# Graph attention layers: GpSimd multiplies the third head's rows of every second group, in place of VectorE

## What is computed

```python
xl = (x @ Wl + bl).reshape(n, h, d)
xr = (x @ Wr + br).reshape(n, h, d)
e = jax.nn.leaky_relu(xl[src] + xr[dst], NEG_SLOPE)
score = jnp.einsum('ehd,hd->eh', e, att)
m = jax.ops.segment_max(score, dst, num_segments=n)
ex = jnp.exp(score - m[dst])
denom = jax.ops.segment_sum(ex, dst, num_segments=n)
alpha = ex / denom[dst]
out = jax.ops.segment_sum(alpha[:, :, None] * xl[src], dst, num_segments=n)
```

## Time and profile before

| | us |
|---|---|
| time, median of 3 runs (lowest to highest) | 6554.96 (6551.42 to 6558.74) |
| the profiled execution, its own time | 6546.25 |
| span in its profile | 6544.4 |
| first graph attention layer, about | 1636 to 3290 |
| second graph attention layer, about | 3390 to 5100 |

### The profile page before, as it was taken

How to read it: one execution, slowest core, us unless ns; L and a number is a source line. 1 busy time by engine, 2 the same in 40 slices (tenths; PEclk the granted TensorE clock), 3 DMA queues, 4 the chain that set the end, 5 groups by cost and what they waited for, 6 DMA issues and landing times. The chain is left out here.

```text
span 6544.4 us, 130007 instructions
## 1 busy us (share of the span) xinstructions
PE 4986.5 (76%) x23046; PEld 2906.8 (44%) x23047; DVE 5557.6 (85%) x13086; ACT 4324.9 (66%) x19265; POOL 3959.7 (61%) x3547
## 2 busy tenths in 40 slices
PE   3796899842888889888878899889998645555663
PEld 2573455421444444444463444444444435555552
DVE  9999988732999999999857999999999547777777
ACT  5576799720899999999837999999999430000001
POOL 0588877785666666666405666666665017777774
PEclk9999999966999999999989999999999767777776
DMA  0362000132555555555515555555556024444444
GB/s 13 62 81 22 2 2 2 11 53 52 146 139 139 140 139 139 140 139 140 100 41 144 140 140 140 139 141 141 139 139 128 23 67 127 127 126 126 126 126 73
DMA packets 397652, 656.25 MB, mean 100 GB/s; under 512 B 141767, under 2 KB 259461, under 8 KB 397044
## 3 DMA queue, kind: packets, MB, share of 16 engines
q0 software_dynamic: 185888, 481.62, 29.0%
q1 hardware_dynamic: 211540, 172.59, 11.3%
HBM read 617.73 MB, written 33.88 MB: 100 GB/s over the span
## 5 line engine op out<-in xcount | busy, mean ns | idle before, releaser
L1272 POOL DMA_INDIRECT feat_area<-xl_table,feat_area x1856 | 2007.0, 1081 | 1476.7 <-PE bank L1346 668.4
L1423 ACT ACTIVATE feat_area<-feat_area 128x130 f32<-128x130 f32 x5568 | 1643.5, 297 | 237.2 <-DVE feat_area L1476 234.0
L1333 PE MATMUL bank<-node_area,feat_area 128*128 x3712 | 1472.3, 520 | 339.4 <-DVE feat_area L1468 174.4
L1407 ACT ACTIVATE feat_area<-feat_area 128x128 f32<-128x128 f32 x4640 | 1442.1, 387 | 30.7 <-issue 30.7
L1346 PE MATMUL bank<-feat_area 128*128 128x390 f32 x3712 | 1408.9, 502 | 33.7 <-ACT feat_area L1407 12.6
L634 POOL DMA_INDIRECT rec_by_dst<-feat_area,gather_col x800 | 1051.2, 1314 | 243.7 <-issue 233.1
L1856 POOL DMA_INDIRECT feat_area<-kv_table,feat_area x832 | 829.4, 997 | 562.3 <-DMA feat_area<-gather_src 309.0
L1333 PEld LDWEIGHTS bank<-node_area,feat_area 128*128 128x128 f32 x3712 | 634.7, 190 | 988.8 <-issue 731.1
L1423 ACT ACTIVATION_READ_ACCUMULATOR feat_area<-feat_area 128x1 f32 x5568 | 1040.2, 187 | 0.0
L1346 PEld LDWEIGHTS bank<-feat_area 128*128 128x128 f32 x3712 | 670.2, 190 | 601.6 <-issue 196.0
L1468 DVE TENSOR_TENSOR feat_area<-bank,feat_area 128x780 f32<-128x780 f32 x928 | 889.6, 959 | 24.4 <-DMA feat_area<-xl_table,feat_area 17.8
(11 more groups left out here) (320 smaller groups left out, 6823.2 us busy)
## 6 DMA issues: line engine op xcount, KB each, us to landing
feat_area<-lo_slot SPq DMA_DIRECT2D x464, 128.0 KB, 3.3
feat_area<-xl_table,feat_area POOLq DMA_INDIRECT x1856, 3.4
feat_area<-lo_slot_src SPq DMA_DIRECT2D x208, 128.0 KB, 3.3
node_area<-lo_edge SPq DMA_DIRECT2D x100, 256.0 KB
xl_table<-feat_area SPq DMA_DIRECT2D x98, 195.0 KB, 3.3
feat_area<-kv_table,feat_area POOLq DMA_INDIRECT x832, 3.0
rec_by_dst<-feat_area,gather_col POOLq DMA_INDIRECT x800
feat_area<-gates SPq DMA_DIRECT2D x348, 32.0 KB
```

The lines of the kernel that those rows point to most:

```text
L1272: pool.indirect_dma_start(ring[:, at:at + HE], None, k.xl, bass.IndirectOffsetOnAxis(ap=index[s // CG][:, n:n + 1], axis=0)).then_inc(gath ...
L1333: last = nc.tensor.matmul(pair[s % 2][:, u, 0:HE], pick[s // 2 % 2][:, c:c + P], k.node[:, ds(columns[0], HE)], start=True, stop=True)
L1407: last = nc.scalar.activation(row[:, 0:D], row[:, 0:D], ACT.Copy, scale=row[:, D:D + 1])
L1423: last = nc.scalar.activation(at, at, ACT.Copy, accum_out=score[s // CG][:, to:to + 1])
```

## The change

VectorE's step `weight` goes, and the same multiplication, on the same rows, is written as a second step of GpSimd's stream with the same lead of -11. GpSimd waits for `weights` there, and raises `byvec`. VectorE's list loses the entry and is otherwise as before.

```diff
-            pipeline(pool, groups, [(0, gather)], U)
+            def weight(j, s):
+                if s % 2:
+                    return
+                pool.wait_ge(weights, chunk(j, s) + 1)
+                pool.nop(nofuse=True)
+                rows = ring4[:, s * GS:(s + 1) * GS, H - 1, :]
+                nc.gpsimd.tensor_tensor(rows[:, :, 0:D], rows[:, :, 0:D], rows[:, :, D:D + 1].to_broadcast([P, GS, D]),
+                                        ALU.mult).then_inc(byvec, 1)
+
+            pipeline(pool, groups, [(0, gather), (-11, weight)], U)
...
-            def weight(j, s):
-                if s % 2:
-                    return
-                dve.wait_ge(weights, chunk(j, s) + 1)
-                rows = ring4[:, s * GS:(s + 1) * GS, H - 1, :]
-                nc.vector.tensor_tensor(rows[:, :, 0:D], rows[:, :, 0:D], rows[:, :, D:D + 1].to_broadcast([P, GS, D]),
-                                        ALU.mult).then_inc(byvec, 1)
...
-                                   (-2, carry), (0, weigh), (-2, spread_fwd), (-3, spread_weights), (-11, weight),
+                                   (-2, carry), (0, weigh), (-2, spread_fwd), (-3, spread_weights),
```

## The result

The changed kernel takes 7185.1 us (median; 7182.1 to 7187.5), the kernel before, run beside it, 6553.6 us: a ratio of 1.097, 95% interval 1.0956 to 1.0983. It is slower by some 631 us. The forecast was 7145 us in a range of 6930 to 7450.

The account below looks back on a forecast made before the run. VectorE was taken to bound the kernel, with ScalarE close behind. A net loss of 3.99 us plus 1.2 of late effects per chunk, over 114 chunks, made 593 us: about 7145 us, in a range of 6930 to 7450.

Parts of the forecast that it names:

- The deciding term: GpSimd's in-order stream: it stands 8.9 us per chunk for the weights, holding group 220's gathers; VectorE loses 5.35 us.
- First leg: From VectorE's weights copy to the addition of the chunk's 12th group after its first: 6.95 us in place of 1.60.
- the gap before it: On GpSimd, between the weights being there and its multiplication: 0.30 us.
- The landing: From the end of a group's second gather on GpSimd to VectorE's addition: 3.1 us, between 2.12 and 3.77.
- What comes late next: TensorE at half clock after idling, and GpSimd starting the chunk late: together 1.2 us per chunk, of 0 to 2.5.
- The part ascribed to GpSimd starting late: GpSimd needs 32.1 us per chunk against VectorE's 31.4, nearly level, so small waits would appear.
- What VectorE gives up: VectorE loses four multiplications of 0.34 us per chunk, 1.36 us, 158 us in all, all on the path.
- The sum: Net 3.99 plus 1.2 gives 5.2 us per chunk, paid by 114 chunks: 593 us, about 7145 us in all.
- the second term: The late effects on TensorE's clock and GpSimd's start, 1.2 us per chunk, added to the net 3.99.
- GpSimd as the bound: Rival: GpSimd's load sets the pace from about 2.8 us a group; 7390 us at 3.1; chance 0.23.
- The two engines in each other's way: Rival: VectorE and GpSimd exclude each other on SBUF reads, up to 3.3 us per chunk, about 7520; chance 0.05.
- Signs that were named: One GpSimd idle stretch per chunk, 114 gather waits of 4 to 6 us, VectorE's busy time down about 80 us per layer.

Follow-up runs that it names:

- wait_only: The kernel before, VectorE keeping its multiplication; GpSimd only waits for the weights at the place of the change's multiplication: 8213.8 us, ratio 1.100.
- lead14: The changed kernel with GpSimd's multiplication three groups later in its stream: 7491.6 us, ratio 1.0027 to the kernel before.
- after_here: The changed kernel, unchanged, run again on another chip: 7181.3 us, ratio 1.0979 to the kernel before there.
- filled2: The changed kernel with five more matmuls of no use on TensorE over the wait, beside the changed kernel on the same chip: 7090.6 us, ratio 1.0832.
- no_mult: The kernel before without the multiplication of the third head's rows in even groups, on any engine: 7383.2 us, ratio 0.9889.
- all14: The changed kernel, multiplication three groups later and on GpSimd in every group, odd ones in place of ScalarE: 7673.3 us, ratio 1.0105 to the kernel before.
- lead13: The changed kernel with GpSimd's multiplication two groups later in its stream: 7610.7 us, ratio 1.0035 to the kernel before.
- work_only: The kernel before, VectorE keeping its multiplication, plus 464 GpSimd multiplications on data of its own without waiting for weights: 7642.9 us, ratio 1.0234.
- lead12: The changed kernel with GpSimd's multiplication one group later in its stream: 7933.0 us, ratio 1.0462 to the kernel before.
- before_here: The kernel before, unchanged, profiled on a slower chip of the experiments: 7482.5 us in one run, 27.58 and 27.70 us per chunk.
- filled: The changed kernel with five more matmuls of no use on TensorE over the wait, on a slower chip: 8268.5 us, ratio 1.0892.

## Why the prediction was right

**The deciding term held.** GpSimd stood 8.7 us before the multiplication of a chunk (8.9 forecast), and VectorE paid for it at one group per chunk. wait_only has the loss with no work, lead14 has the work and next to no loss (0.27%).

**First leg, the sum of 6.95 us.** Measured 6.47 in the mean. In the chunk shown: 0.23 + 0.15 + 0.62 + 0.18 + 1.08 + 0.31 + 0.95 + 2.66 = 6.18. Two terms were sized too high: the multiplication (0.82; it takes 0.62) and the gap before it (0.30; 0.15). The landing, 2.90 us in the mean over a layer's 57 such gathers, was near the 3.1 taken.

**What comes late next, 1.2 us of 0 to 2.5.** This was the mis-sized term. With all of the 1.36 us granted, leg two is 7.76 where 6.62 - 0.34 = 6.28 was due, 1.5 us more, most of it the clock as the fill of the pipeline had shown (1.85 there; 1.1 by after_here and filled2). Leg three is 18.89 where 19.33 - 1.02 = 18.31 was due: 0.6 more. Together 2.1, not 1.2; the 0.6 is about what no_mult gives back too little. The part ascribed to GpSimd starting late was small in the change itself (38 us of waits at other groups than the fifth, 17 before) and came out only when the clock no longer hid it.

**What VectorE gives up, 1.36 us.** It was priced too high, and that "all of it" is on the path did not hold: on its own it is worth 0.76 us (no_mult), with ScalarE close behind VectorE. In the changed kernel it can't be separated from leg three.

**The sum.** +5.2 us per chunk forecast, +5.6 and +5.8 measured; too little in the second term, too much in the first and in the landing, so that the 7145 came within 40 us of 7185 partly by luck, by errors that cancel.

**The rivals.** GpSimd as the bound: it had 0.23 and is not what happened, as all14 shows even with twice the work. The two engines in each other's way: real, but not in the change as it was made. There L1485 takes 962 ns against 959 before: 302 of the 464 multiplications start while VectorE executes nothing, the second of a chunk in its wait for the gather (L1477), the third in its wait for the sums (L1511), and only 8 start under L1485. Of VectorE's lines L1462 grew by 31 us over the kernel and L1592 by 19. It counts only once the wait is gone, and then it takes the whole saving. In expecting 6400 to 6460 us of lead14 (on the scale of the first measurement) I had left it out, and that expectation failed, as did lead13's.

**Signs that were named.** One idle stretch of GpSimd per chunk, 115 waits of L1477 at one group per chunk, 4.5 us each, L1588 every 33.1 and 33.3 us (32 to 33 forecast), L1342 at its half-clock length of about 2.96 us after 113 of the 114 waits: all there. VectorE's busy time fell by 63 us in all, not by 80 in each layer: L1462 and L1592 grew by 50, and I take the rest to be instructions whose ends had overlapped with the next and now end in front of a wait.

No version tried beats the kernel before. The nearest, lead14, is 0.27% slower. The two ends of the trade are a saving of 0.8 us per chunk and a price of at least as much in VectorE's other instructions.

## What to carry to other kernels

An engine's idle time is only worth something at the place in its stream where the new work would stand: look there for the moment at which the operand exists, and at what is queued behind. An instruction with a wait, put in front of gathers that run ahead, ends their running ahead; three groups later in the same stream the same work cost 0.27%. And before arithmetic moves from VectorE to GpSimd, subtract what VectorE's other instructions will lose beside it, those with two operands in SBUF above all.

## What the runs showed of the hardware

- GpSimd's two-operand multiplication of 128 x 256 fp32 took 623 ns in the median where VectorE mostly stood (the change; 605 at the least, in all14), VectorE's 419. Beside VectorE's work it took 706 (all14) to 1003 ns (work_only) in the mean and 2447 at the most (lead14).
- What it cost VectorE hung on what it met: with four per chunk VectorE's other instructions grew by 1.5 us at three lines in work_only, 1.3 in lead14 and lead13, but only by 0.5 in the change (after_here) and 0.2 in lead12; with eight by 0.8 in all14 (durations of all of them, per chunk, against before_here). Writes alone cost them nothing.
- An idle stretch of TensorE of 5.15 us was followed by eight matmul instructions at half the clock; five matmuls of no use in that stretch were worth 91 us of the whole.
- Chips differed by 14 to 16% in this kernel's time, nearly all of it outside the layers, and by 1.2 to 1.4 us per chunk for the one stalling kernel measured on two (filled, filled2), while a chunk of the kernel before took the same to 0.12 us.
